# In the gelu slot TensorE does the value piece first and the temperature network's second product behind it

## What is computed

```
scores = (Q K^T) / 4                                   # per batch and head, 112 x 375
feats  = [mean(scores), mean(rowmax(scores)), mean(var(softmax(scores)))]    # 3 per head
hidden = gelu(feats W1^T + b1); hidden = gelu(hidden W2^T + b2)
t      = exp(clip(hidden w3^T + b3))                   # one temperature per batch and head
attn   = softmax(Q K^T / (2 t)) V
x      = x + tanh(g) * (attn Wo^T + bo)
```

## Time and profile before

| | us |
|---|---|
| median of 3 runs | 973.49 |
| lowest, highest | 972.94, 976.38 |
| the profiled execution, whole | 977.35 |
| its span, first to last instruction | 974.7 |
| its mean granted PE clock | 0.916 of full |
| busy in the span: PE, DVE, ACT, POOL | 771.2, 767.1, 742.5, 427.5 |

### The profile page before, as it was taken

The page is one execution under the profiler, slowest core; times in us unless marked ns, Lnnn a source line. Parts: engine busy times, 40 slices in busy tenths (PEclk is TensorE's granted clock), DMA queues, the critical chain, the costliest instruction groups (busy, mean ns, idle before and its releaser), DMA issues. The chain is left out here.

```text
span 974.7 us, 22484 instructions
## 1 busy us (share of the span) xinstructions
PE 771.2 (79%) x7426; PEld 531.9 (55%) x7426; DVE 767.1 (79%) x1676; ACT 742.5 (76%) x1549; POOL 427.5 (44%) x874
## 2 busy tenths in 40 slices
PE   2546898899989999898899989898888404777776
PEld 1223566676666666666666666666656302444444
DVE  1649888897989879898897989888761338999996
ACT  1125689888898888889888888887876408999995
POOL 5455565756557575665757556572121100000000
PEclk8658799998999989999998999998898857999997
DMA  9686646765768665676665667655000190000001
GB/s 220 130 150 144 125 75 110 143 100 101 128 109 130 115 120 107 112 125 110 136 114 101 122 110 124 114 110 80 16 21 11 51 252 0 20 24 24 26 26 34
DMA packets 111409, 94.26 MB, mean 97 GB/s; under 512 B 26111, under 2 KB 107711, under 8 KB 111295
## 3 DMA queue, kind: packets, MB, share of 16 engines
q1 hardware_dynamic: 111310, 93.00, 50.4%
HBM read 42.72 MB, written 12.85 MB: 57 GB/s over the span
## 5 line engine op out<-in xcount | busy, mean ns | idle before, releaser
L635 ACT ACTIVATE pt<-p_t,ct 125x336 f32<-125x336 f32 x512 | 250.4, 546 | 66.8 <-PE p_t L810 64.7
L545 DVE BATCH_NORM_STATS2 stats<-ex 112x6 f32<-112x375 f32 x512 | 253.9, 539 | 43.8 <-ACT ex L645 42.7
L645 ACT ACTIVATE ex<-p_s,nm 112x375 f32<-112x375 f32 x512 | 268.6, 590 | 19.0 <-DVE nm L564 19.0
L564 DVE TENSOR_REDUCE nm<-p_s 112x2 f32<-112x750 f32 x256 | 237.5, 928 | 19.9 <-PE p_s L696 19.7
L810 PEld LDWEIGHTS p_t<-qst,kst 99*125 99x125 bf16 x1536 | 128.9, 141 | 59.0 <-issue 20.8
L810 PE MATMUL p_t<-qst,kst 99*125 99x112 bf16 x1536 | 146.0, 227 | 12.4 <-ACT pt L635 9.8
L696 PE MATMUL p_s<-kst,qst 96*112 96x375 bf16 x512 | 135.0, 347 | 25.7 <-ACT ex L645 22.5
L783 PE MATMUL p_m<-ctxt,wk_sb 128*128 128x375 f32 x256 | 105.4, 536 | 19.9 <-DMA ctxt<-ctxt_dram 14.7
L766 PE MATMUL p_m<-wv_sb,ctxt 128*125 128x256 f32 x384 | 113.0, 420 | 2.6 <-DVE on L533 1.1
L713 PE MATMUL p_o<-pt,va 125*32 125x112 f32 x3072 | 105.3, 272 | 1.3 <-ACT pt L635 0.8
L713 PEld LDWEIGHTS p_o<-pt,va 125*32 125x32 f32 x3072 | 73.0, 113 | 39.5 <-issue 33.4
(11 more groups left out here) (140 smaller groups left out, 1252.0 us busy)
## 6 DMA issues: line engine op xcount, KB each, us to landing
kst<-kp SPq DMA_DIRECT2D x384, 93.8 KB, 4.2
ctxt<-ctxt_dram SPq DMA_DIRECT2D x32, 375.0 KB, 3.5
qbounce<-qp SPq DMA_DIRECT2D x32, 168.0 KB, 3.9
qst<-qbounce SPq DMA_DIRECT2D x32, 168.0 KB, 2.7
xa<-x_dram SPq DMA_DIRECT2D x32, 112.0 KB, 3.7
qst<-qbounce SPq DMA_DIRECT2D x32, 112.0 KB, 2.7
xm<-x_dram SPq DMA_DIRECT2D x32, 112.0 KB, 3.0
x_dram<-x SPq DMA_DIRECT2D x32, 112.0 KB, 2.7
```

Source lines behind the costliest of these rows:

```text
L545: last = nc.vector.bn_stats(stats[:, nb % RING, 2 * pb + i], ex[:, 2 * (t % 2) + i, :])
L564: nc.vector.tensor_reduce(nm[:, n % RING, 2 * p:2 * p + 2], p_s[t % 2][0:SQ, :, 0:SK], axis=AX.X, op=ALU.max, negate=True).then_inc(s_max, 1)
L635: nc.scalar.activation(pt[:, (2 * r + i) % 8], p_t[i][0:KR, 0:KC * SQ].rearrange("k (c q) -> k c q", c=KC), ACT.Exp, scale=ct[0:KR, nr % R ...
L645: last = nc.scalar.activation(ex[:, 2 * ((t - 1) % 2) + i, :], p_s[(t - 1) % 2][0:SQ, i, 0:SK], ACT.Exp, bias=nm[:, ne % RING, h:h + 1])
```

## The change

PE issues the wait for `hid1` and the second product after all projection pieces of the slot, and so behind V2, not ahead of it. No other engine's program changes, and no instruction or transfer is added or removed.

```diff
-                if p == 7 and pair_of(n):
-                    pe.wait_ge(s_g1, n // 2)
-                    mm(t_h2, w2t[:, :], hid1[:, :], start=True, stop=True).then_inc(s_h2, 1)
-
                 if p == 0 and active("Q", n):
...
                         last = nc.tensor.transpose(p_m[0:SQ, g4 * P:(g4 + 1) * P], oa[:, g4, :], ident[:, :])
                     last.then_inc(s_ob, 1)
+                if p == 7 and pair_of(n):
+                    pe.wait_ge(s_g1, n // 2)
+                    mm(t_h2, w2t[:, :], hid1[:, :], start=True, stop=True).then_inc(s_h2, 1)
                 if weighted and p == 7:
                     if pair_of(n):
                         pe.wait_ge(s_g2, n // 2)
```

## The result

The changed kernel takes 981.77 us (median of 5 runs, 980.19 to 983.53), the kernel before 973.06 (5 runs, 970.96 to 976.38): 8.7 us more, ratio 1.0086, 95% interval 1.0061 to 1.0111. It is slower, and by more than the 0.5% that the prediction held a measurement to be able to tell. Executions that took over 1.5% more than the fastest of their kernel (two of q_early, 988.37 and 988.50, and one of the kernel before, 1007.47) are left out of the ratios and ranges. The profiled execution of the changed kernel took 980.19 us, with a span of 978.3.

What follows compares the result with a forecast made beforehand. PE, DVE and ACT, each 85 to 90% busy, bound the kernel, with ACT's chain setting gelu slots. Falls removed -6.3, added +19, last slot -1.0: +11.7 on 973.49 gives 985.2 us; range 970 to 996.

Steps and rivals of the forecast that it cites:

- The second product and ACT's chain, 0: Gelu slot: V2 just fits the gap, the second product still starts at 317.00, ACT's chain stays: cost 0.
- The idle time of PE is split, not removed: Gelu slot: PE's idle 0.86 us moves partly behind the second product; 1.08 us idle before the transposed scores, formerly 0.46.
- The three shares in the prediction: PE's idle time in the gelu slot: 0.06 before the second product, 0.37 before `pv`, 0.62 more before the transposed scores.
- DVE's copy of V2: Gelu slot: the copy comes some 1.2 us earlier, while DVE waits for ACT anyway: 0.
- More falls, later and dearer: Behind V2, a longer thin part: 10 clock falls of 13 at 1.9 us, +19, replacing 4 at 1.58, -6.3.
- the proportion's 6.5: Steady gelu slots: falls counted in proportion to the thin part's length, 4 x 3.9 / 2.4 = 6.5 of 13.
- The last gelu slot, -1.0: Last gelu slot: V2, formerly 2.07 us at the low clock, goes into the gap: about -1.0 us, once.
- The sum: Whole kernel: -6.3 for removed falls, +19 for added ones, -1.0 for the last gelu slot: +11.7 us.
- Nothing moves: Rival: gelu slot's second product, ACT's chain and clock falls stay as now; 972.5 to 975.3 us; chance 0.20.
- The clock holds: Rival: V2 fills the gap that makes the falls, so all four vanish; -7.3, 966.2 us; chance 0.11.
- The second product late: Rival: slow V2 delays ACT 0.11 to 1.05 us in 16 gelu slots, +1.8 to +16.8; chance 0.07.

Runs made afterwards that it cites:

- q_early: The changed kernel with the Q piece of the next slot 0 moved into the gelu slot, behind `pv`: 978.4 us, ratio to the kernel before 1.0036.
- fill_large: The changed kernel plus two large products (128x256, result unread) behind `pv` in gelu slots that have a next Q piece: 970.36 us, ratio to the kernel before 0.9963.
- fill_small: The changed kernel plus eight small products (64x32, result unread) behind `pv` in gelu slots with a next Q piece: 984.12 us, ratio to the kernel before 1.0087.
- before_fill: The kernel before plus two large products (result unread) in the gap ahead of the second product: 965.16 us, ratio to the kernel before 0.9911.
- split_v2: The changed kernel with the second product issued between two halves of V2, nothing added: 984.45 us, ratio to the kernel before 1.0124.
- late_second: The changed kernel plus one large product (128x256, result unread) ahead of V2, making the second product late: 985.44 us, ratio to the kernel before 1.0134.

## Why the prediction was right, and where its sizes were off

*The second product and ACT's chain, 0.* Right, and shown twice: the same 1.97 us from table load to second gelu, and the same 497.86 us of steady part in both orders with the clock held.

*The idle time of PE is split, not removed.* Right: 0.37 and 1.07 us were measured for 0.37 and 1.08 (0.46 and 0.62). The three shares in the prediction, 0.06, 0.37 and 0.62, add up to 1.05 and not to 0.86; V2 takes less time in the gap than it took behind the second product (1.03 us against 1.13 in the rows), so PE idles somewhat more in all. DVE's copy of V2 came 0.96 us earlier (2.07 us after the table load, not 3.03), not 1.2, which cost nothing.

*More falls, later and dearer.* The mechanism is right, and fill_large, fill_small and before_fill together show that it is the clock, and large work, that decide it. The sizes were off. I took 10 falls and there are 7; going to the middle between 6.5 and all 13 had no ground. That the proportion's 6.5 lies close to 7 may be luck: no run tests that the count grows with the length of the thin part, split_v2 with two shorter ones has eight, and in after the falls simply come behind every second gelu slot. I took them to start 5.5 us behind the table load and they start at 6.7 (the last one at 4.7). I took 1.9 us each, the mean of a short and a long one, and a long one costs 2.40, and six of seven are long: 6.8 us at 0.35 us for each, against 0.38 worked out from before.

*The last gelu slot, -1.0.* Right in the slot, but little of it is left at the end. V2 runs at the full clock there (1.10 us, not 2.07), and the transposed scores come 4.15 us after the table load (738.11 - 733.96), where it was 5.20 (735.12 - 729.92). From its table load to the end of the span it is 974.7 - 729.92 = 244.78 before, 978.3 - 733.96 = 244.34 after: -0.4.

*The sum.* Inside the steady part lie five long falls and the short one, whose table loads are 42.59 us apart, and three of before's: 5 x 2.40 + (42.59 - 41.46) - 3 x 1.58 = +8.4, where the rows give +8.15; the rest is that distances with the clock held are 0.02 to 0.03 us shorter in after (41.46, not 41.48 or 41.49). The last counted fall of either kernel lies behind the steady part, and from there to the end of the span the two take 323.93 and 324.06 us. So +8.3 in all, where 8.7 was measured between the medians and 11.7 predicted. The prediction added 19 for falls where the steady part has 13.1, and took off 6.3 for those of before where it has 4.7. Too many falls and too small a price for each partly made up for each other, so that the total came out nearer than the count did.

*The rivals.* "Nothing moves" was right in all but the clock. "The clock holds" was half right: V2 in the gap does remove the falls that began inside V2 (none of the seven does), but what V2 leaves behind makes others. "The second product late" did not happen; late_second shows that it would have cost its full amount.

What stays open: why the falls come behind every second gelu slot (191.36, 276.68, 362.02 and so on, 85.33 us apart), what makes a product large enough, why the times ahead of and behind the steady part differ by some 6 us each from kernel to kernel (142.95 to 148.95, and 319.7 to 325.6), and why q_early spreads over 14 us. No run here was made for any of them.

## What to carry to other kernels

When a wait is hidden by moving a large product in front of it, look at what the large product leaves behind: on a kernel whose engines all run at 85 to 90%, a stretch of small products can cost the clock of the next slots, and no wait in the stretch itself shows it. Work out the price from table-load to table-load distances (or any other landmark of a period) with the clock held and fallen. If a whole large product of real work can be laid on both sides of the small products, from a slot whose neighbours are dense, do that; giving away the piece of the very next slot only moves the hole.

## What was not expected of the hardware

TensorE's clock fell with the engine busy: in fill_small PE had 1.11 us of small products (64x32) in place of its idle time, and the granted clock was 0.5 at 155.58 us all the same, while 1.13 us of large ones (128x256) in the same place held it at 1.00 for 497.86 us. And two halves of one piece, 0.6 and 0.7 us on either side of the second product, held it no better than the whole piece behind or ahead of it: falls behind 8 of 13 gelu slots, against 4 and 7, and a ratio of 1.0124 to before, where after has 1.0086.
